# Which banks the turned keys and the weighed values take, in a six-layer local attention

## The reference, cut to what matters

```
qkv = shift_tokens(x) @ Wqkv[i];  q, k, v = split(qkv, 3)
q = l2norm(q) * qs;  k = l2norm(k) * ksc
q = q * cos * scale + rotate_half(q) * sin * scale
k = k * cos / scale + rotate_half(k) * sin / scale
# each query sees its own block of 32 and the block before
attn = softmax(where(mask, -big, q @ k.T * 8))
x = (attn @ v) @ Wo + x
x = ffn_layer(shift_tokens(x)) + x      # layer norm, 341 hidden, gated gelu
```

## Time and profile before

| | |
|---|---|
| median of three runs | 4887.78 us |
| profiled execution | 4899.51 us, span 4897.4 |
| local transformer, first to last step | some 3200 us, from about 500 to 3780 |
| TensorE, VectorE busy over the span | 86%, 74% |
| ScalarE, GpSimd busy over the span | 52%, 58% |

### The profile page before, as it was taken

The page is one execution under the profiler, slowest core; times in us unless marked ns, Lnnn a source line. Parts: engine busy times, 40 slices in busy tenths (PEclk is TensorE's granted clock), DMA queues, the critical chain, the costliest instruction groups (busy, mean ns, idle before and its releaser), DMA issues. The chain is left out here.

```text
span 4897.4 us, 167150 instructions
## 1 busy us (share of the span) xinstructions
PE 4225.8 (86%) x70698; PEld 3385.6 (69%) x70890; DVE 3638.9 (74%) x5894; ACT 2546.2 (52%) x3896; POOL 2850.0 (58%) x2141
## 2 busy tenths in 40 slices
PE   6996899999998999999999999999998658668667
PEld 6885677777777777777777777777775338658447
DVE  4444888888888888888888888888885564564554
ACT  2232456655555555665556555565554326546435
POOL 2223777777777777777777777777773027517025
PEclk9776999999999999999999999999999868868878
DMA  0001222222222322222222222222221021221022
GB/s 24 0 0 38 74 63 62 67 77 70 63 62 61 85 69 62 62 79 72 63 63 66 78 62 68 64 66 66 66 66 36 9 58 43 73 59 44 23 61 74
DMA packets 214198, 281.51 MB, mean 57 GB/s; under 512 B 58878, under 2 KB 103716, under 8 KB 212740
## 3 DMA queue, kind: packets, MB, share of 16 engines
q1 hardware_dynamic: 203972, 251.85, 19.9%
q0 software_dynamic: 9536, 19.55, 1.5%
HBM read 54.88 MB, written 18.28 MB: 15 GB/s over the span
## 5 line engine op out<-in xcount | busy, mean ns | idle before, releaser
L1524 POOL TENSOR_TENSOR local_rot<-local_rot,local_sines 128x512 f32<-128x512 f32 x768 | 955.2, 1277 | 889.4 <-DVE local_sines L1603 889.4
L1532 POOL TENSOR_TENSOR local_inv_norm<-local_norm2c,minus_half 128x16 f32<-128x16 f32 x384 | 1126.6, 2934 | 31.9
L1411 ACT COPY local_v_tile<-local_bank 128x1024 f32<-128x1024 f32 x192 | 195.0, 1016 | 755.1 <-PE local_bank L1186 755.1
L1184 PE MATMUL local_bank<-local_wqkv_hi,local_ys_hi 128*128 128x512 f32 x1152 | 493.2, 428 | 24.8 <-POOL local_ys_lo L1515 10.4
L1260 PE MATMUL local_bank<-ident,local_normed 128*128 128x128 f32 x3072 | 405.9, 275 | 105.7 <-ACT local_probs_t L1421 90.1
L1603 DVE TENSOR_TENSOR local_rot<-local_bank,local_table 128x1024 f32<-128x1024 f32 x384 | 467.1, 1216 | 11.3 <-issue 7.0
L1593 DVE TENSOR_TENSOR local_normed<-local_rot,local_inv_norm 128x1024 f32<-128x1024 f32 x384 | 454.7, 1218 | 19.4 <-issue 11.5
L1603 DVE TENSOR_TENSOR local_sines<-local_bank,local_table 128x1024 f32<-128x1024 f32 x384 | 466.5, 1215 | 0.0
L1608 DVE TENSOR_REDUCE local_norm<-local_squares 128x16 f32<-128x1024 f32 x384 | 463.9, 1209 | 0.0
L1186 PE MATMUL local_bank<-local_wqkv_hi,local_ys_lo 128*128 128x512 f32 x1152 | 455.2, 395 | 0.0
L1185 PE MATMUL local_bank<-local_wqkv_lo,local_ys_hi 128*128 128x512 f32 x1152 | 455.2, 395 | 0.0
(11 more groups left out here) (420 smaller groups left out, 9074.9 us busy)
## 6 DMA issues: line engine op xcount, KB each, us to landing
local_vals<-local_v_tile SPq DMA_DIRECT2D x1152, 130.0 KB
local_vals<-local_v_tile SPq DMA_DIRECT2D x672, 65.0 KB
local_stage<-in_L_ffn_Wqkv SPq DMA_DIRECT2D x6, 1536.0 KB, 7.1
moe_w<-y_rows SPq DMA_DIRECT2D x32, 256.0 KB, 5.1
moe_w<-in_L_ffn_W SPq DMA_DIRECT2D x3, 2048.0 KB, 9.9
x_rows<-moe_rows SPq DMA_DIRECT2D x12, 512.0 KB, 4.0
local_wo<-in_L_ffn_Wo SPq DMA_DIRECT2D x6, 512.0 KB
moe_taken<-x_rows,moe_take POOLq DMA_INDIRECT x149, 2.6
```

Source lines behind the costliest of these rows:

```text
L1184: nc.tensor.matmul(out, hi, wqkv_hi[:, d0:d1], start=True, stop=False)
L1524: last = nc.gpsimd.tensor_tensor(of_heads(rot, a)[:, :, to], of_heads(rot, a)[:, :, to], of_heads(sines, a)[:, :, of], ALU.add)
L1532: nc.gpsimd.tensor_tensor(inv_norm[:, cols], norm2c[:, cols], g.minus_half[:, cols], ALU.pow).then_inc(q["inv_norms_ready"], 1)
```

## The change

The turned keys go to banks 4 and 5 in place of 0 and 1. The first half of the weighed values goes to 0 and 1, the second to 4 and 5. The waits follow the banks: the keys' turning waits until VectorE has multiplied the next queries (`products_ready` with part 1), the first half no longer waits for that, and where there is no next tile, the last tiles wait for the division. `att_ready` is counted twice a tile, once for each half: the next scores wait for the first half only, the next queries' projection and the turn of the output for both. On VectorE the second half's division comes after the keys' sum of squares and after the projected output of k-1 was added.

```diff
-    QK, QK_TURN = ((4, 5), (6, 7)), ((2, 3), (0, 1))
-    WEIGHED, WO_BANK = ((4, 5), (0, 1)), 2
+    QK, QK_TURN = ((4, 5), (6, 7)), ((2, 3), (4, 5))
+    WEIGHED, WO_BANK = ((0, 1), (4, 5)), 2
...
-                    "sums_inverted": 2, "att_ready": 1, "y_added": 1,
+                    "sums_inverted": 2, "att_ready": 2, "y_added": 1,
...
                 def make_scores(m):
                     pe.wait_ge(q["qkt_copied"], tile("qkt_copied", m))
-                    pe.wait_ge(q["att_ready"], tile("att_ready", m - 1))
+                    pe.wait_ge(q["att_ready"], tile("att_ready", m - 1, 1))
...
                         pe.wait_ge(q["v_copied"], tile("v_copied", m))
                         pe.wait_ge(q["out_copied"], tile("out_copied", m - 2))
+                    elif is_tile(m + 1):
+                        pe.wait_ge(q["products_ready"], tile("products_ready", m + 1, 1))
                     else:
-                        pe.wait_ge(q["probs_t_ready"], tile("probs_t_ready", m - 1))
+                        pe.wait_ge(q["att_ready"], tile("att_ready", m - 2))
...
                         pe.wait_ge(q["probs_t_ready"], tile("probs_t_ready", m))
-                        if is_tile(m + 2):
-                            pe.wait_ge(q["products_ready"], tile("products_ready", m + 2, 1))
                     elif is_tile(m + 1):
                         pe.wait_ge(q["qkt_copied"], tile("qkt_copied", m + 1))
+                    else:
+                        pe.wait_ge(q["att_ready"], tile("att_ready", m - 1))
...
-                    for i in range(2):
-                        dve.wait_ge(q["pv_done"], tile("pv_done", m, i + 1))
...
-                    last.then_inc(q["att_ready"], 1)
+                def divide(m, i):
...
+                    nc.vector.tensor_tensor(att[:, i * 512:(i + 1) * 512]..., weighed[:, :, :, 0:HD],
+                                            inv_sum[:, i]..., ALU.mult).then_inc(q["att_ready"], 1)
...
                     if is_tile(k):
-                        divide(k)
+                        divide(k, 0)
                     if is_tile(k + 2):
                         sum_squares(k + 2, 1)
                     if is_tile(k - 1):
                         add_output(k - 1)
+                    if is_tile(k):
+                        divide(k, 1)
```

More of the change, by code:

```diff
@@ L1608, in sum_squares @@
                     nc.vector.tensor_reduce(norm2[:, cols], of_heads(squares, a), AX, ALU.add).then_inc(q["norms_ready"], 1)
-                def divide(m):
-                    def weighed(i):
-                        return bank[:, WEIGHED[i][0]:WEIGHED[i][1] + 1, 0:4 * (HD + 1)].rearrange("p a (c d) -> p a c d", d=HD + 1)
-                    for i in range(2):
-                        dve.wait_ge(q["pv_done"], tile("pv_done", m, i + 1))
[L1617 to L1622, removed]
-                    last.then_inc(q["att_ready"], 1)
+                def divide(m, i):
+                    weighed = bank[:, WEIGHED[i][0]:WEIGHED[i][1] + 1, 0:4 * (HD + 1)].rearrange("p a (c d) -> p a c d", d=HD + 1)
+                    dve.wait_ge(q["pv_done"], tile("pv_done", m, i + 1))
+                    nc.vector.reciprocal(inv_sum[:, i].unsqueeze(3), weighed[:, :, :, HD:HD + 1]).then_inc(q["sums_inverted"], 1)
+                    dve.wait_ge(q["sums_inverted"], tile("sums_inverted", m, i + 1))
+                    if i == 0:
+                        dve.wait_ge(q["out_turned"], tile("out_turned", m - 1))
+                    nc.vector.tensor_tensor(att[:, i * 512:(i + 1) * 512].rearrange("p (c a d) -> p a c d", a=2, d=HD), weighed[:, :, :, 0:HD],
+                                            inv_sum[:, i].unsqueeze(3).to_broadcast([P, 2, 4, HD]), ALU.mult).then_inc(q["att_ready"], 1)
                 def add_output(m):
```

## The result

The changed kernel takes 4826.16 us, the median of four runs (4821.07 to 4834.84); the kernel before took 4888.63 beside it (four runs, 4876.82 to 4897.02). The ratio is 0.9876, 95% interval 0.985 to 0.9901: faster by 62 us. The forecast was 21 us faster, with a range whose lower end, 4852, the result passes by 26. The profiled execution took 4834.8 us (span 4832.9), 64.7 less than that of before.

What follows compares the result with a forecast made beforehand. TensorE, busy 16.19 of 16.65 us, bounds steps through scores, D and keys. (0.21 + 0.21) x 47 sequences = 19.7 us, plus 1.6 at five layer starts, is 21.3 off 4887.8: 4867, range 4852 to 4884.

Steps and rivals of the forecast that it cites:

- Keys into banks 4 and 5: TensorE's keys wait for D, not ScalarE's copy; they start 0.21 us sooner in each step of kinds 3 and 0.
- D: End of VectorE's second product of the next queries with cosines and sines; keys were forecast to start 0.14 us later.
- Kinds 3 and 0: Steps with k modulo 4 equal to 3 or 0, 16.65 us each; forecast 16.44, the main gain.
- kinds 1 and 2: Steps with k modulo 4 equal to 1 or 2, 17.26 and 15.66 us; together forecast to keep 32.9.
- VectorE's wait at the reciprocal: VectorE's 0.78 us wait for the second half goes, but moves to its wait for scores; worth 0.
- Rival D: VectorE's wait at the reciprocal, 129.5 us in all, was on the path and most goes: 4758; chance 0.05.
- GpSimd sets the stretch from kind 1 to kind 2: GpSimd's rotation, sequence reading and inversions fix D to D at 17.73 us whatever TensorE does; gain 0.
- Rival B: GpSimd's chain is the bound in all steps, so nothing moves: 4888; chance 0.08.
- rival C: Release of TensorE's keys from VectorE takes over 0.35 us after D, so slower: 4905 at 0.53; chance 0.05.
- the sentence on the halves: Next scores need only the first half divided, next queries' projection both; neither waits, so no gain was counted.
- Rival A: Time won returns as longer holes in TensorE's scores, from the pace of instructions; half given back, 4877; chance 0.12.
- the row of 34.1 us: TensorE's idle time amid score matmuls with no cause named: 38 times in 3000 us, 0.9 us each.

Runs made afterwards that it cites:

- Kernel 1: Changed kernel with the keys' turning again also waiting for ScalarE's copy of the turned weights: 4856.25 us, ratio 0.9932 to the kernel before.
- kernel 4: Changed kernel with VectorE's old order and the next scores waiting for both halves, so only the new banks are left: 4865.77 us, ratio 0.9948.
- Kernel 3: Changed kernel with VectorE's old order, both halves divided one after the other; the scores still wait for the first half only: 4830.94 us, ratio 0.987.
- kernel 9: Changed kernel with GpSimd splitting the next sequence's input in kind 1 ahead of its rotation, behind VectorE's normalising: ratio 0.9852 to the kernel before.
- kernel 6: Changed kernel with VectorE's feed-forward shift in kind 2 moved ahead of the queries' second product: 4816.44 us, ratio 0.9847.
- kernel 2: Changed kernel with the next scores waiting for both divided halves again: 4925.69 us, ratio 1.0071 to the kernel before.
- 10: Changed kernel with both the earlier GpSimd split of kernel 9 and the earlier VectorE shift of kernel 6: ratio 0.9797 to the kernel before.
- kernels 2 to 5: The fifth is the kernel before with only VectorE's new order, old banks and scores behind both halves: 4949.05 us, ratio 1.0109.

## Why the prediction was right and wrong

*Keys into banks 4 and 5: right in place and in size.* The keys start 0.14 us behind D, the value taken. Kinds 3 and 0 have 16.44 and 16.45, forecast 16.44; kinds 1 and 2 together keep 32.9. Kernel 1 puts the old wait back and loses 30 us, of which regular steps account for 19; kernel 4, with the banks and without the relaxed wait of the scores, gains 27 us, forecast 21. That its 4865.77 stands beside the forecast's 4867 is in part luck, as the kernel before took 4892.77 there.

*VectorE's wait at the reciprocal: right.* It is gone, and the wait for scores is longer by 0.68 in the step shown and by as much in kind 1 (medians 0.39 and 1.03), 0.5 to 0.6 forecast; in kind 2 VectorE has no such wait. Kernel 3 puts the order back and changes nothing. Rival D falls.

*GpSimd sets the stretch from kind 1 to kind 2: right*, D to D 17.7 before and after, 17.1 in kernel 9, and still 17.7 in kernel 6, which shortened kind 2 without touching GpSimd and gave it back in kind 3. Rival B, that it sets all kinds, falls with the steps of 16.44, and rival C with the 0.14.

*The step that failed* is the sentence on the halves: "The next scores now need only the first half divided, and the next queries' projection needs both: with 3 us of scores and values between them neither waits." It asked whether anybody waits, found that nobody does, and so priced the relaxed wait at nothing. Kernels 3 and 4 differ in that wait alone and are 35 us apart; kernel 2 against the changed kernel gives 100, where 30.0 are a plain wait for the second half and the holes over all kinds grow from 17.8 to 58.3 us. TensorE's matmuls never waited for the halves in the steps looked at. Its queue did, in all 139 steps of kinds 0, 1 and 2, and behind that wait stood the instructions that were to be fetched. The size missed is 35 us by these two kernels, which with the 21 forecast makes 56 of the 62. The rest, some 6 us, is about the spread of one kernel's runs, and I have no separate cause for it.

*Rival A had the right row and the wrong sign.* It asked whether holes come from the pace of instructions, and let them only grow. It was 12% of the chance and gave 4877; the row of 34.1 us that it rested on was also something that the change could remove, and no rival said so. In kernels 6, 9 and 10 something like it is at work: of a gain in kind 2 54 to 71% comes back as a longer kind 3. In kernel 9 nearly all of that is holes (16 us of 17), in 6 and 10 about half (11 of 26 and 18 of 35), the rest being the longer wait for D. In the changed kernel itself kind 3's holes shrank, from 27.8 to 17.8.

On fetching, the Trainium skill's page "Runtime: NRT & Kernel Launch", section "Instruction fetch mechanics", has 16 KiB blocks of 256 instructions, brought by a queue of the sequencer's own, and their crossing "mostly hidden". The blocks agree with the trace (8.93 MB in 545 packets of the instruction queue, 16.4 KB each; holes at one count modulo 256). "Mostly hidden" is true here of most borders, but 49 others in the scores of the kernel before cost 0.2 to 2.3 us each, 46.5 us in all.

*What stays open.* That a late wait makes the fetch late is shown by the distances and by the starts of the transfers; what inside the sequencer starts a transfer isn't seen, nor why it lies about 1.2 us behind the wait. Why the matmuls go on no sooner than 2.2 us behind its start isn't either. In kernels 2 to 5 more time is won and lost than the holes in the scores and the named waits add up to (before to after 40 and 28.7; from the changed kernel to kernel 2 100, where a wait of 30.0 and 40.5 of holes are named), which I haven't traced to single instructions. No kernel moved L1202 ahead of the turn back, so why kind 3 keeps its holes, and why they grow in kernels 6, 9 and 10, wasn't tried.

## What to carry to other kernels

A wait that nobody seems to stand at can still cost: ask when the queue passes it, and how dense the instructions behind it are; put waits early, or weaken them, ahead of a dense stretch of short instructions. A row of idle time with no cause is a term of the sum with both signs, and its bound (here 34.1 us in 38 times) belongs in the range on the faster side too. A gain in one step is worth what the next one keeps of it: kernel 6 took 0.9 us from kind 2 and kind 3 got 0.9 longer. Before work is moved to an idle spot of GpSimd, look at what VectorE runs beside it.

## What the runs showed of the hardware

- TensorE runs dry at borders of 256 instructions when 128 small matmuls and their weight loads follow a wait that was passed up to 2.1 us before (once, in kernel 6, 2.45); in none of the changed kernel's 136 scores with 2.65 us or more did it. The holes are 0.2 to 2.3 us before and after (the longest, in kernel 2, 4.4) and end 2.2 to 3.0 us behind the start of the instruction transfer (one at 3.5).
- The transfer at such a hole began 1.20 to 2.08 us behind the passing of that wait (28 holes of the kernel before).
- VectorE and GpSimd operations that both read two SBUF inputs meet at a price to both: two 128x1024 multiplications 4.18 us for 2.35, the second of two 64x512 subtractions 2.04 us for 1.17.
- From VectorE's end to TensorE's transposes that wait for it: 0.145 to 0.147 us in 183 steps of the changed kernel, the same as from ScalarE's end in the earlier trace rows.
